# Four layers in one kernel: instruction queues reordered, tap sums taken by GpSimd, context banks swapped, and a folded query weight for two images

## The reference, cut to what matters

```python
# layer 0: attention over the 256 pixels, width 128
out = softmax((t @ Wq.T + bq) @ (t @ Wk.T + bk).T / sqrt(128)) @ (t @ Wv.T + bv) @ Wo.T + bo
# layer 1: batch norm, sign, grouped 3x3 conv with sign weights, batch norm, residual, PReLU
# layer 2: depthwise 3x3 conv, norm, relu, prune channels with a small maximum,
#          pointwise 128x128 conv, norm, relu, prune
# layer 3: linear attention, 8 heads of 16
q, k, v = split(w_qkv @ xf);  k = softmax(k, over pixels)
context = k @ v.T (per head);  out = w_out @ (context.T @ q) + b_out
```

## Time and profile before

| | |
|---|---|
| median of 3 runs | 71.0 us (70.77, 71.0, 71.87) |
| profiled execution | 70.44 us, of which the span of the core's instructions 68.7 us |
| instructions | 2001 |
| busy in the span: PE, DVE, ACT, POOL | 61.9, 42.9, 33.3, 32.3 us |
| granted TensorE clock over the span | 1.00 |
| chain that ended last, on PE | 66% of the span |

### The profile page before, as it was taken

How to read it: one execution, slowest core, us unless ns; L and a number is a source line. 1 busy time by engine, 2 the same in 40 slices (tenths; PEclk the granted TensorE clock), 3 DMA queues, 4 the chain that set the end, 5 groups by cost and what they waited for, 6 DMA issues and landing times.

```text
span 68.7 us, 2001 instructions
## 1 busy us (share of the span) xinstructions
PE 61.9 (90%) x727; PEld 47.6 (69%) x727; DVE 42.9 (62%) x165; ACT 33.3 (49%) x104; POOL 32.3 (47%) x98
## 2 busy tenths in 40 slices
PE   3996979999999999979998899799999997999940
PEld 2772759889999756658885567266767796998710
DVE  3959865767755946794359950093839786564450
ACT  5201783966987220084047870060462498774600
POOL 5805684889998547670030004417407559242000
PEclk9999999999999999999999999999999999999999
DMA  0897220000000000000000000000000000002032
GB/s 0 174 410 201 41 40 2 0 0 0 10 0 0 5 0 14 0 0 0 0 0 0 5 10 0 0 10 0 0 10 0 0 0 0 0 14 76 0 134 95
DMA packets 2778, 2.14 MB, mean 31 GB/s; under 512 B 976, under 2 KB 2512, under 8 KB 2768
## 3 DMA queue, kind: packets, MB, share of 16 engines
q1 hardware_dynamic: 2768, 2.01, 10.2%
HBM read 1.49 MB, written 0.52 MB: 29 GB/s over the span
## 4 chain that ended last, share of the span: by engine, by line
PE 66%; issue 10%; DVE 6%; DMA 5%; POOL 4%; ACT 4%; SPq 1%
PE bank L1510 9%; PE bank L1449 6%; PE bank L1407 5%; PE bank L1436 5%; DMA x<-in_x 5%; PE bank L1562 3%; PE bank L1621 3%; PE bank L1383 3%; PE bank L1641 3%; PE bank L1595 3%; PE bank L1418 3%; PE bank L1586 3%; PE bank L1576 3%; PE bank L1323 2%; PE bank L1395 2%
## 5 line engine op out<-in xcount | busy, mean ns | idle before, releaser
L1323 PE MATMUL bank<-warm 128*128 128x256 bf16 x59 | 9.7, 316 | 1.1 <-POOL warm L356 1.1
L372 POOL TENSOR_TENSOR gn_rstd<-gn_var_eps,minus_half 128x1 f32<-128x1 f32 (+2 forms) x12 | 7.4, 615 | 4.2 <-DVE gn_var_eps L862 3.4
L1510 PE MATMUL bank<-x,dw_diag 32*32 32x256 f32 x288 | 8.9, 376 | 0.3 <-DVE x L1108 0.3
L1323 PEld LDWEIGHTS bank<-warm 128*128 128x128 bf16 x59 | 6.5, 118 | 3.4 <-POOL warm L356 1.1
L1510 PEld LDWEIGHTS bank<-x,dw_diag 32*32 32x32 f32 x288 | 5.3, 103 | 2.2 <-issue 0.9
L1449 PE MATMUL bank<-signs,conv_blocks 128*128 128x256 bf16 x36 | 4.3, 276 | 0.4 <-ACT signs L641 0.4
L641 ACT ACTIVATE signs<-res,bn_shift,bn_scale 128x256 bf16<-128x256 f32 x4 | 2.2, 593 | 4.8 <-issue 4.8
L1465 PE MATMUL bank<-valid,dw_diag 32*32 32x256 f32 x72 | 4.5, 377 | 0.0
L1407 PE MATMUL bank<-k,q 128*128 128x256 f32 x16 | 4.2, 387 | 0.2 <-ACT q L608 0.2
L1145 DVE TENSOR_SCALAR_CACHE_REDUCE h_linear<-bank,dw_scale 128x256 f32<-128x256 f32 x4 | 1.9, 481 | 4.0 <-PE bank L1538 4.0
L483 POOL TENSOR_TENSOR gn_mean_squared<-gn_group 128x2 f32<-128x2 f32 x2 | 0.5, 240 | 8.3 <-DVE gn_group L1128 8.3
(11 more groups left out here) (197 smaller groups left out, 159.3 us busy)
## 6 DMA issues: line engine op xcount, KB each, us to landing
out<-x SPq DMA_DIRECT2D x4, 128.0 KB, 1.7
late_params<-in_late SPq DMA_DIRECT2D x1, 404.5 KB, 4.6
x<-in_x SPq DMA_DIRECT2D x1, 384.0 KB, 3.6
early_params<-in_early SPq DMA_DIRECT2D x1, 258.0 KB, 3.8
x<-in_x SPq DMA_DIRECT2D x1, 128.0 KB, 2.2
pw_weights<-in_late SPq DMA_DIRECT2D x2, 64.0 KB, 3.5
pw_weights<-in_late SPq DMA_DIRECT2D x4, 32.0 KB, 1.9
l_params<-in_late SPq DMA_DIRECT2D x4, 2.2 KB, 1.7
```

The costliest lines, as they stand in the source:

```text
L372: return nc.gpsimd.tensor_tensor(out_ap, in_ap, minus_half[:, 0:n], ALU.pow)
L1323: nc.tensor.matmul(bank[:, 0:N], warm[:, 0:C], warm[:, :], start=True, stop=True)
L1510: nc.tensor.matmul(tile_of(p, i, r), dw_diag[of, tap, :], xs[2][of, 2 * p + i, dy:dy + H, dx:dx + W], start=(tap == 0), stop=False)
```

## The change

- **Valid sum.** The mask, its 72 matmuls and the copy of the result go. GpSimd forms nine sums of taps (tap_sums, six operations on 128x3) after the head masks, and ACT spreads them over valid_sum in four pieces (corners, two kinds of edges, inside) after the four signs. less_mean waits for four pieces.
- **Channel statistics of x1.** They move from GpSimd (four steps) to VectorE (three steps, x1_channel_mean and x1_channel_var) between group_var(1, 2) and group_out(1, 3).
- **Fillers.** In place of the taps, 3 stand ahead of group_means(1, 3), and 22 instead of 10 ahead of the conv; the 13 ahead of pointwise(1) become 7.
- **Folded query.** TensorE transposes the query weight of layer 3 once, before the conv, into bank 0. For images 0 and 1 q is not projected any more: fold_query multiplies the query weight into the projected context (in bank 0), ACT copies it (fold_out), and output multiplies it with t3. Images 2 and 3 still project q, in bank 0, after the copy of fold 0 and 1.
- **Banks.** The context of images 0 and 2 is in bank 3, that of 1 and 3 in bank 7.
- **Orders.** ACT: q_out(0) and v_out(0) earlier among the diagonals, v3_out(0) ahead of norm3_first(1), the last stage rearranged. GpSimd: mean_diag ahead of gn2_scale. VectorE: row_max(1) ahead of k_out(2), group_out(3, ...), norm3(0) earlier, norm3(3) ahead of k3_max(2), x3_out(3) ahead of k3_max(1). TensorE: scores(1) two projections earlier, group_means2(0) after tap 2, group_means3(0) before the last tap, project_v3(0) and project_k3(0) ahead of pointwise(1), and the last stage rearranged.

```diff
 late_warm_ps = banks[6]
 gap_warm_ps = banks[5]
 l2_row_ps = banks[4][:, N:N + C]
+wq3_ps = banks[0][:, 0:C]
+fold_ps = banks[0][:, 0:C]
 k3_ps = [banks[(6, 2)[b % 2]][:, 0:N] for b in range(B)]
 vt_ps = banks[5][:, 0:N]
 kt_ps = banks[1][:, 0:N]
 pj_ps = banks[4][:, 0:C]
 y_ps = [banks[(6, 2)[b % 2]][:, 0:N] for b in range(B)]
 gn_ps = banks[7]
-cx_ps = [banks[(7, 3)[b % 2]][:, 0:C] for b in range(B)]
+cx_ps = [banks[(3, 7)[b % 2]][:, 0:C] for b in range(B)]
...
         nc.gpsimd.tensor_tensor(mv[:, 1, b, 0:1], x1_sum[:, b, 0:1], x1_sum[:, b, 1:2],
                                 ALU.add).then_inc(x1_sum_ready, 1)
-    def x1_channel_stats():
-
-        pool.wait_ge(x1_sum_ready, B)
-        pool.wait_ge(x1_square_ready, B)
-        step(nc.gpsimd.tensor_scalar(bn1_m[:, :], mv[:, 1, :, 0], 1.0 / N, 0.0, ALU.mult, ALU.add))
-        nc.gpsimd.tensor_scalar(bn1_e[:, :], mv[:, 1, :, 2], 1.0 / N, 0.0, ALU.mult, ALU.add)
-        step(nc.gpsimd.tensor_tensor(bn1_msq[:, :], bn1_m[:, :], bn1_m[:, :], ALU.mult))
-        nc.gpsimd.tensor_tensor(bn1_v[:, :], bn1_e[:, :], bn1_msq[:, :],
-                                ALU.subtract).then_inc(x1_channel_ready, 1)
-
     def sw_root():
         pool.wait_ge(sw_var_ready, 1)
         root(sw_rstd[:, :], sw_var[:, :]).then_inc(sw_rstd_ready, 1)
...
         nc.gpsimd.tensor_scalar(limit2[:, :], l2_shift[:, 2:3], -1.0, PW_THRESH,
                                 ALU.mult, ALU.add).then_inc(l2_consts, 1)
-    def valid_mask():
-        step(nc.gpsimd.memset(valid[:, :, :], 0.0))
-        nc.gpsimd.memset(valid[:, 1:H + 1, 1:W + 1], 1.0)
+    def sum_mask():
         nc.gpsimd.tensor_scalar(group_sum[:, :], group_avg[:, :], 1.0 / N, 0.0,
                                 ALU.mult, ALU.add).then_inc(sum_masks, 1)
+    def tap_sums():
+        pool.wait_ge(late_in, 16)
+        taps = lp[:, LC["dw"]].rearrange("p (y x) -> p y x", y=3)
+        rows, sums = tap_rows, tap_sum
+        nc.gpsimd.tensor_tensor(rows[:, 0, :], taps[:, 1, :], taps[:, 2, :], ALU.add)
+        step(nc.gpsimd.tensor_tensor(rows[:, 2, :], taps[:, 0, :], taps[:, 1, :], ALU.add))
+        step(nc.gpsimd.tensor_tensor(rows[:, 1, :], rows[:, 2, :], taps[:, 2, :], ALU.add))
+        nc.gpsimd.tensor_tensor(sums[:, :, 0], rows[:, :, 1], rows[:, :, 2], ALU.add)
+        step(nc.gpsimd.tensor_tensor(sums[:, :, 2], rows[:, :, 0], rows[:, :, 1], ALU.add))
+        nc.gpsimd.tensor_tensor(sums[:, :, 1], sums[:, :, 2], rows[:, :, 2],
+                                ALU.add).then_inc(tap_sum_ready, 1)
     def group_swaps():
...
         pool.wait_ge(bn_var_ready, i + 1)
         root(bn_rs[:, i:i + 1], bn_ve[:, i:i + 1]).then_inc(bn_rstd_ready, 1)
-    valid_mask()
+    sum_mask()
     other_roots()
     sw_root()
     l2_constants()
...
     x1_sums(2)
     gn_root(1, 1)
     x1_sums(3)
-    x1_channel_stats()
     gn_root(1, 2)
     gn_root(1, 3)
     bn_root(0)
     group_swaps()
     head_masks()
+    tap_sums()
     bn_root(1)
+    gn2_mean_diag(0)
     gn2_scale(0)
-    gn2_mean_diag(0)
+    gn2_mean_diag(1)
     gn2_scale(1)
-    gn2_mean_diag(1)
     out_bias_less_floor(0)
     x3_sum_less_floor(0)
     out_bias_less_floor(1)
...
         nc.scalar.activation(dw_diag[:, tap, :], ident_tile[:, :], ACT.Copy,
                              scale=lp[:, at:at + 1]).then_inc(dw_diag_ready, 1)
-    def valid_taps_out():
-        act.wait_ge(valid_mm, 1)
-        nc.scalar.activation(valid_sum[:, :], valid_ps, ACT.Copy, scale=-1.0).then_inc(valid_ready, 1)
+    def valid_sum_out():
+        act.wait_ge(tap_sum_ready, 1)
+        image = valid_sum[:, :].rearrange("p (h w) -> p h w", h=H)
+        edge, inside = slice(0, H, H - 1), slice(1, H - 1)
+        for y, high in ((edge, 2), (inside, H - 2)):
+            for x_at, wide in ((edge, 2), (inside, W - 2)):
+                sums = tap_sum[:, 0:3:2, :] if high == 2 else tap_sum[:, 1:2, :]
+                sums = sums[:, :, 0:3:2] if wide == 2 else sums[:, :, 1:2]
+                nc.scalar.activation(image[:, y, x_at], sums.to_broadcast([C, high, wide]),
+                                     ACT.Copy, scale=-1.0).then_inc(valid_ready, 1)
     def q_out(b):
...
                              accum_out=sum3[:, b:b + 1]).then_inc(e3_ready, 1)
     def q3_out(b):
-        act.wait_ge(q3_mm, b + 1)
+        act.wait_ge(q3_mm, b - 1)
         nc.scalar.activation(q3[:, b, :], q_ps, ACT.Copy).then_inc(q3_done[b], 1)
+    def query_weights_out():
+        act.wait_ge(wq3_mm, 1)
+        nc.scalar.activation(wq3[:, :], wq3_ps, ACT.Copy).then_inc(wq3_ready, 1)
+    def fold_out(b):
+        act.wait_ge(fold_mm, b + 1)
+        nc.scalar.activation(folded[:, b, :], fold_ps, ACT.Copy).then_inc(fold_ready[b], 1)
     def v3_out(b):
         act.wait_ge(vt3_mm, b + 1)
...
     dw_diagonal(2)
     dw_diagonal(3)
     setup_out()
+    q_out(0)
     dw_diagonal(4)
+    v_out(0)
     dw_diagonal(5)
     dw_diagonal(6)
-    q_out(0)
-    v_out(0)
     q_out(1)
     softmax(0)
     v_out(1)
...
     l2_diagonal()
     x1_square(2)
     x1_square(3)
+    query_weights_out()
     sign_out(0)
-    valid_taps_out()
     sign_out(1)
     sign_out(2)
     sign_out(3)
+    valid_sum_out()
     conv_less_mean(0)
     conv_less_mean(1)
     bn2_diagonal()
...
     square_sum3(1)
     relu1(1, 0)
     relu1(1, 1)
+    v3_out(0)
     norm3_first(1)
-    v3_out(0)
-    q3_out(0)
+    softmax3(0)
+    kt3_out(0)
     square_sum3(2)
-    softmax3(0)
     square_sum3(3)
-    kt3_out(0)
     softmax3(1)
     v3_out(1)
-    q3_out(1)
     kt3_out(1)
     project_out(0)
+    fold_out(0)
     softmax3(2)
     v3_out(2)
     kt3_out(2)
     softmax3(3)
+    project_out(1)
     v3_out(3)
+    fold_out(1)
     kt3_out(3)
-    project_out(1)
     project_out(2)
     q3_out(3)
...
+    def x1_channel_mean():
+        dve.wait_ge(x1_sum_ready, B)
+        step(nc.vector.tensor_scalar(bn1_m[:, :], mv[:, 1, :, 0], 1.0 / N, None, ALU.mult),
+             "bn1_m")
+        settle("bn1_m")
+        step(nc.vector.tensor_tensor(bn1_msq[:, :], bn1_m[:, :], bn1_m[:, :], ALU.mult),
+             "bn1_msq")
+    def x1_channel_var():
+        dve.wait_ge(x1_square_ready, B)
+        settle("bn1_msq")
+        step(nc.vector.scalar_tensor_tensor(
+            out=bn1_v[:, :], in0=mv[:, 1, :, 2], scalar=1.0 / N, in1=bn1_msq[:, :],
+            op0=ALU.mult, op1=ALU.subtract), "bn1_v")
     def bn1_mean_sq():
         dve.wait_ge(group_read[1], B)
-        dve.wait_ge(x1_channel_ready, 1)
         step(nc.vector.tensor_tensor(bn1_dev[:, :], bn1_m[:, :], gs[:, 1, :, 0], ALU.subtract),
              "bn1_dev")
         dve.wait_ge(var_ready[1], B)
...
         step(nc.vector.tensor_tensor(bn1_dev_sq[:, :], bn1_dev[:, :], bn1_dev[:, :], ALU.mult),
              "bn1_dev_sq")
         settle("bn1_dev_sq")
+        settle("bn1_v")
         step(nc.vector.tensor_tensor(bn1_sq[:, :], bn1_dev_sq[:, :], bn1_v[:, :], ALU.add),
              "bn1_sq")
         settle("bn1_sq")
...
     k_out(1)
     norm0(3)
     rinv_out(0)
+    row_max(1)
     k_out(2)
     sw_scale()
     sw_products()
-    row_max(1)
     k_out(3)
     row_max(2)
     rinv_out(1)
...
     norm1(0)
     group_var(1, 1)
     x1_out(3)
+    group_out(1, 2)
     norm1(1)
-    group_out(1, 2)
     group_var(1, 2)
+    x1_channel_mean()
+    x1_channel_var()
     group_out(1, 3)
     group_var(1, 3)
     bn1_mean_sq()
...
     prune1_max(0, 1)
     prune1_weights(0, 1)
     prune1_max(0, 0)
+    prune1_weights(0, 0)
     means2(1)
-    prune1_weights(0, 0)
     prune2_max(0)
     prune2_floor(0)
     prune2_max(1)
     x3_out(0)
     prune2_floor(1)
     x3_out(1)
+    group_out(3, 0)
+    group_var(3, 0)
     prune1_max(1, 1)
-    group_out(3, 0)
+    group_out(3, 1)
+    norm3(0)
+    group_var(3, 1)
     prune1_weights(1, 1)
-    group_var(3, 0)
     prune1_max(1, 0)
-    group_out(3, 1)
     prune1_weights(1, 0)
-    group_var(3, 1)
-    norm3(0)
+    k3_max(0)
     prune2_max(2)
     prune2_floor(2)
     prune2_max(3)
     x3_out(2)
     prune2_floor(3)
-    k3_max(0)
     x3_out(3)
     k3_max(1)
     group_out(3, 2)
     group_var(3, 2)
+    context_out(0)
     group_out(3, 3)
     group_var(3, 3)
     norm3(2)
-    context_out(0)
+    norm3(3)
     k3_max(2)
-    norm3(3)
     context_out(1)
     k3_max(3)
+    q3_out(2)
     x4_out(0)
     context_out(2)
-    q3_out(2)
     context_out(3)
     x4_out(1)
...
-    def valid_taps(tap):
-
-        if tap == 0:
-            pe.wait_ge(sum_masks, 1)
-            pe.wait_ge(exp_ready, 2 * 3)
-        pe.wait_ge(dw_diag_ready, tap + 1)
-        dy, dx = tap // 3, tap % 3
-        for r in range(TILES):
-            of = slice(r * TILE, (r + 1) * TILE)
-            ins = nc.tensor.matmul(valid_ps[of], dw_diag[of, tap, :],
-                                   valid[of, dy:dy + H, dx:dx + W],
-                                   start=(tap == 0), stop=(tap == TAPS - 1))
-        if tap == TAPS - 1:
-            ins.then_inc(valid_mm, 1)
-
```

(95 more changed lines are left out.)

7 lines of the change are left out of this document (2 added, 5 removed).

## The result

The changed kernel took 71.52 us (median of 8; 71.16 to 74.53) beside 70.77 us for the kernel before (median of 8), a ratio of 1.0125 with a 95% interval of 1.0101 to 1.0148. By the ratio that is a loss of 0.9 us, and within 2%; the forecast was 71.1 us with a range of 69.3 to 72.4. Measured a second time (after_again, the same kernel) the ratio was 1.0099 (1.0080 to 1.0119), a loss of 0.7 us. Some executions of every kernel here take 1 us or more longer than the rest; the ratios leave them out, and the profile of head_only (70.4 us) is of such an execution. The profiled execution took 71.32 us with a span of 69.6 us.

The account below looks back on a forecast made before the run. The kernel was taken as bound by TensorE's order of work, with a latency-bound stretch before the first sign. Terms -0.20 - 1.05 + 1.34 = +0.09 on a 71.0 us median gave 71.1 us, range 69.3 to 72.4.

Parts of the forecast that it names:

- Attention: From the query copy to attend(3): earlier scores(0), partly lost to a stall before scores(1); gain 0.2 us (0 to 0.45).
- Statistics: Layer 1's statistics up to the first sign: group means no longer queue behind valid taps; gain 1.05 us (0.7 to 1.2).
- The second rival: Layer 1: the statistics gain fails, by late channel steps or a longer scores(1) stall; 72.0, up to 72.8 us; chance 0.10.
- The clock: TensorE ahead of the conv: 1.5 us idle after 22 fillers; clock loss possible, but no term in the sum.
- the rival: Ahead of the conv: after the 1.5 us gap the array runs at 1.2 GHz; 73 to 75 us, chance 0.04.
- Depthwise: Conv to depthwise: earlier group means and mean_diag remove the wait before less_mean(0); gain 0.6 us (0.35 to 0.7).
- Up to pointwise(1): Depthwise taps to pointwise(1): group_means3(0) and image 0's projections come first; 0.1 us left of the 0.6 (-0.1 to 0.4).
- The last stage: Third layer's end: TensorE's order queues context(3) behind fold_query(1), project_q3(3) and output(1); loss 1.4 us (0.4 to 1.8).
- The fold takes 0.42 of matmul time away: Last stage: two query projections of 0.43 us removed, two folds of 0.22 added; an argument for the first rival.
- the first rival: Last stage: the tail is no worse than before, so earlier gains stand; 69.4 us, or 69.0 to 70.2; chance 0.27.

Follow-up runs that it names:

- head_only: The change up to and with less_mean(1), with the last stage of the kernel before; 68.87 us, 0.9771 of the kernel before.
- scores1_back: The changed kernel with scores(1) behind the projections of image 2 and row_max(1) behind k_out(2), as before; 70.79 us, 1.0060 of the kernel before.
- stats_gpsimd: head_only with scores(1) and row_max(1) in their old places and x1's channel statistics again four GpSimd steps; 68.99 us, 0.9769 of the kernel before.
- fillers_2: The changed kernel with 2 in place of 22 fillers ahead of the conv; 72.73 us, 1.0316 of the kernel before.
- unfolded_covered: ctx3_early without the fold, q of images 0 and 1 projected again in TensorE's waits for statistics; 69.39 us, 0.9841 of the kernel before.
- ctx3_early: The changed kernel with context(3) and project_context(2) ahead of fold_query(1), project_q3(3) and output(1), ACT's copies moved to match; 70.15 us, 0.9956 of the kernel before.

## Why the prediction was right, and which terms were off

The mechanism was as forecast: a gain at the statistics and in the depthwise conv, given back by TensorE's order in the last stage. The total of +0.1 came out as +0.9 and +0.7, by errors of which the large ones have one sign: 0.2 in attention and 0.5 in the last stage. The profiles show the same sum: the sign 1.10 earlier and the rest 1.84 longer, 0.74 lost, and 0.15 more from the start of this execution. That 71.1 stands only 0.4 below the measured 71.52 is in part luck: it was added to a base of 71.0, and the eight runs of the kernel before have 70.77.

- **Attention: forecast 0.20 gained, measured 0.** scores(0) came 0.24 earlier (9.58 for 9.82) although TensorE's first projection started some 0.15 later in this execution (7.13 for 6.99; this start differs from profile to profile, from 6.84 to 7.60 in the variants), so 0.39, near the 0.45 of the text. The stall ahead of scores(1) is there, by k_out(1), 12.17 - 11.78 = 0.39 for the 0.3 forecast, and then the timeline is where it was: scores(2) at 15.32 less 0.15 is 15.17 in both kernels. scores1_back puts the price at 0.3 to 0.5. The text allowed for this in its low end of 0, but its middle had each part a little too good: 0.45 for the 0.39 gained; TensorE free at 11.55, where it is 11.63 in the old clock (11.78 - 0.15); k_out(1) done at 11.8, where it is 11.87 (11.54 + 0.48 - 0.15); and nothing for the 0.15 between the end of that copy (12.02) and scores(1) (12.17).
- **Statistics: forecast 1.05, measured 1.10.** The group means started 0.1 after the square sum (24.84 for 24.74), and VectorE's three steps weren't late. head_only's gain and stats_gpsimd bear it out. The sign came 1.10 earlier and not 1.25, because attention added nothing. The second rival asked for group_out(1,3) behind 25.9; it came at 25.32.
- **The clock: no term, and none was needed.** The gap was 1.42 for the forecast 1.5, with a conv of 4.26 us, before 4.28. fillers_2 shows that the rival was one of size: 20 fillers fewer and it costs 1.5 us. The forecast of 73 to 75 was a little high for it; the conv took 5.73 and not up to 8.6, since the clock came back during it.
- **Depthwise: forecast 0.6, measured 0.56.** From depthwise(0,0) to less_mean(0) it was 5.28 (38.62 to 43.90) and is 4.72.
- **Up to pointwise(1): forecast at 13.8 after depthwise(0,0), measured 14.17,** before 13.90. The cut by group_means3(0) cost 0.47 for the 0.4 of the text (less_mean(1) 11.38 after depthwise(0,0), in head_only 10.91). It didn't set the time: the projections of image 0, which stand ahead of pointwise(1), waited for norm3(0), which ended at 13.03 (50.71) for the forecast 12.88 (the text's 51.5 in the old clock). They started at 13.09 (50.77) for 12.93 and held TensorE for 1.08 us instead of 0.90.
- **The last stage: forecast 1.34 from depthwise(0,0) on, measured 1.84** (28.59 for 26.75); this is the term that carries most of the error. Of it the part behind norm3(2) was forecast as 1.70 and came as 1.98; the other 0.22 is norm3(2) itself, 18.97 after depthwise(0,0) for the forecast 18.75, which is what is left of the late pointwise(1). context(3) was forecast for 62.8 in the new clock and came at 63.54. The two waits of 0.5 ahead of output(2) and output(3) were forecast and came. For the idle time ahead of fold_query(1), project_q3(3) and these two the forecast was 1.5 or more; with the matmuls at the text's prices it is 0.31 + 0.18 + 0.67 + 0.67 = 1.83. The 0.89 from project_context's start to the output held to the hundredth (63.98 to 64.87); from project_context(1) to fold_query(1) it was 0.84 (60.81 to 61.65), and from there to project_q3(3) 0.95 (to 62.60).
- **"The fold takes 0.42 of matmul time away"** stood as an argument for the first rival. It is true of the sum (two of 0.43 for two of 0.22), but the saved ones could be covered and the added ones are not: unfolded_covered is 0.8 faster than ctx3_early.

What remains open is the share of each of the other moves on ACT and VectorE in the last stage: head_only, ctx3_early and unfolded_covered settle TensorE's order and the fold, and 69.39 (unfolded_covered) stands 0.5 above head_only's 68.87 with causes I haven't separated.
